# Gathering a table by one-hot matmuls: table rows folded by 2 in place of 4, and a gather queue tied to it from its first gather on

## The reference

```
x = x + relu(ln(x) @ W + segment_sum((ln(x) @ M)[src], dst))          # 200000 edges, sorted by dst
z = ln(x)
h = (z @ W_gat).reshape(N, 4 heads, 4 experts)                        # 16 numbers a node
e = leaky_relu(a_src[src2] + a_dst[dst2])                             # 131072 unsorted edges, and a loop a node
alpha = segment_softmax(e, dst2)
scores = ln(segment_sum(h[src2] * alpha, dst2) + b).mean over heads   # 4 numbers a node
w = softmax(top2(scores))
x = x + sum over experts e of w[e] * (gelu(z @ W1[e] + b1[e]) @ W2[e] + b2[e])
```

## Time and profile before

| | us |
|---|---|
| median of 3 runs | 3602.7 (3602.44 to 3619.45) |
| the profiled execution, its own time | 3607.5 |
| its span, first to last instruction | 3606.3 |
| mean granted TensorE clock in it | 0.872 of full |

### The profile page before, as it was taken

One profiled execution on the slowest core, in us unless ns is written; L12 is line 12 of the kernel. 1 busy time (PEld: TensorE's weight loads), 2 busy tenths in 40 slices (PEclk: granted clock), 3 DMA queues, 4 the chain that ended last, 5 costly groups with the idle time before them and its releaser, 6 DMA issues.

```text
span 3606.3 us, 43520 instructions
## 1 busy us (share of the span) xinstructions
PE 2660.3 (74%) x13434; PEld 1983.9 (55%) x13459; DVE 2198.0 (61%) x5820; ACT 900.2 (25%) x1563; POOL 2364.7 (66%) x2799
## 2 busy tenths in 40 slices
PE   2665767778777777777777877877777888888925
PEld 1443555555545555545555555555555767777824
DVE  6677676677775555465455555555313768787857
ACT  3000111111112222211111111111133545565513
POOL 4666666666666666656666666666888788888540
PEclk9667888879888888989989989989887999999968
DMA  9676665666666666656666666666414112222146
GB/s 289 219 253 201 184 196 183 199 201 193 191 190 205 188 197 196 197 170 200 211 195 215 199 189 215 204 203 210 114 22 120 42 40 54 53 66 52 39 146 225
DMA packets 476805, 601.23 MB, mean 167 GB/s; under 512 B 72486, under 2 KB 415390, under 8 KB 474526
## 3 DMA queue, kind: packets, MB, share of 16 engines
q1 hardware_dynamic: 378766, 375.94, 32.2%
q0 software_dynamic: 97216, 219.88, 22.2%
q10 hardware_dynamic: 592, 2.64, 0.2%
HBM read 313.06 MB, written 286.79 MB: 166 GB/s over the span
## 4 chain that ended last, share of the span: by engine, by line
PE 25%; DVE 22%; another core or an unknown queue 14%; issue 11%; DMA 2%; ACT 2%; POOL 1%; DVEq 0%; SPq 0%; ACTq 0%; POOLq 0%
PE wide L1637 7%; PE wide L1526 6%; DVE ring L834 6%; PE wide L1576 4%; PE wide L1586 4%; DVE one_hot L767 3%; DVE picked L892 2%; DMA ring<-xn_d,srci 2%; DVE low_hot L881 2%; DVE by_row L994 1%; DVE by_row L987 1%; PE wide L1545 1%; POOL ring L1729 1%; PE wide L1682 1%
## 5 line engine op out<-in xcount | busy, mean ns | idle before, releaser
L1729 POOL DMA_INDIRECT ring<-xn_d,srci x1611 | 1556.9, 966 | 913.5 <-DVE ring L834 417.2
L834 DVE SCALAR_TENSOR_TENSOR ring<-ring,same_v,wide 128x256 f32<-128x256 f32 x1610 | 771.3, 479 | 934.2 <-remote 390.7
L1526 PE MATMUL wide<-ring,one_hot 128*128 128x256 f32 x3222 | 971.4, 440 | 402.7 <-DVE ring L834 237.7
L1526 PEld LDWEIGHTS wide<-ring,one_hot 128*128 128x128 f32 x3222 | 673.6, 219 | 653.4 <-DVE ring L834 222.3
L1637 PE MATMUL wide<-tab_parts,low_hot 128*128 128x208 bf16 x6288 | 672.0, 260 | 115.3 <-issue 103.2
L1637 PEld LDWEIGHTS wide<-tab_parts,low_hot 128*128 128x128 bf16 x6288 | 565.9, 100 | 221.5 <-issue 205.0
L1780 POOL DMA_INDIRECT g<-tab_d,srt x500 | 495.4, 991 | 82.6 <-issue 45.3
L1586 PE MATMUL wide<-w2s,hh 128*128 128x256 f32 x1568 | 416.0, 413 | 45.5 <-DVE yo L808 28.1
L1576 PE MATMUL wide<-xt,w1s 128*128 128x512 f32 (+1 forms) x832 | 413.1, 625 | 7.3 <-ACT hh L1255 5.4
L1255 ACT ACTIVATE hh<-wide,b1c 128x512 f32<-128x512 f32 (+1 forms) x208 | 137.8, 662 | 1067.0 <-PE wide L1576 488.5
L1586 PEld LDWEIGHTS wide<-w2s,hh 128*128 128x128 f32 x1568 | 327.1, 210 | 117.9 <-issue 28.1
(11 more groups left out here) (370 smaller groups left out, 1881.5 us busy)
## 6 DMA issues: line engine op xcount, KB each, us to landing
run_d<-ring SPq DMA_DIRECT2D x201, 1024.0 KB
ring<-xn_d,srci POOLq DMA_INDIRECT x1611
y_d<-yo SPq DMA_DIRECT2D x196, 128.0 KB
comb<-y_d SPq DMA_DIRECT2D x28, 896.0 KB
low_row<-low_d SPq DMA_DIRECT2D x13, 1024.0 KB
sum_d<-g SPq DMA_DIRECT2D x15, 768.0 KB
g<-tab_d,srt POOLq DMA_INDIRECT x500
xn_d<-ring SPq DMA_DIRECT2D x7, 896.0 KB, 6.9
```

The source lines that it names most:

```text
L834: dve_at["run", j] = step(V.scalar_tensor_tensor(out=o, in0=ring[:, (j - 1) // JC % RING, (j - 1) % JC, :], scalar=same_v[:, j:j + 1], in1 ...
L1526: mm = T.matmul(bank[pair_bank[p]][:, j % 2 * D:(j % 2 + 1) * D], one_hot[:, j // 4 % 4, j % 4, :], ring[:, j // JC % RING, j % JC, :], st ...
L1729: G.indirect_dma_start(out=ring[:, s, j % JC, :], out_offset=None, in_=xn_d, in_offset=at_rows(srci[:, j:j + 1])).then_inc(sem(f"gather{s} ...
```

## The change

- The low part of a node number becomes 8 bits (256 rows, two halves of 128 lanes), the high part runs over 25 values (`HI` = 25). A column takes 3 parts x 2 halves = 6 matmuls of 400 = 16 x 25 table columns, into one bank of its own.
- All one-hots of the low part come from ACT: two halves a block, two instructions each of 512 columns, as many as before. `low_columns` on DVE is gone.
- `pick` takes half a block (two columns, two banks, 2 x 16 x 25 sums), so it runs twice a block, in the first and the third turn. Four halves (two blocks) can be open in PSUM; PE waits twice a block for a pick of two blocks before. The semaphore `picked` counts halves.
- `high_hot` has 25 entries a column and is an 8-bit integer.
- The lock: every gather from number 56 on waits, the first for 8 halves (4 blocks), the last for 237 (118.5 blocks).
- In the end stage a pause stands ahead of each of the second part's 28 gathers.
- SP loads a tile's register once and keeps it: for the stores of `x1_d` and `tab_d` (49 each) it uses the one that `fetch` loaded, and for `y_d` it loads with the first expert alone. PE no longer waits for `one_hot` from visit 8 on.

```diff
-    HI = -(-NT // 4)
-    LOW = 4 * P
+    HI = -(-NT // HALVES)
+    LOW = HALVES * P
+    WIDE = 4 * P
...
-    high_hot = r.take("high_hot", [P, NTC, HI], BF16)
+    high_hot = r.take("high_hot", [P, NTC, HI], U8)
...
-    low_hot = q.take("low_hot", [P, DEPTH, 4, LOW], BF16)
-    picked = q.take("picked", [P, 4, HX, HI], F32)
+    low_hot = q.take("low_hot", [P, DEPTH, HALVES, WIDE], BF16)
+    picked = q.take("picked", [P, 2, HX, HI], F32)
...
-        def low_columns(b):
-
-            c = chunk_of[b]
-            V.wait_ge(sem(f"low_in{c % 2}"), sent(c // 2))
-            if b >= DEPTH:
-                V.wait_ge(sem("picked"), b - DEPTH + 1)
-            at = block_in[b] * LOW
-            for q_ in range(4 - ACT_QUARTERS):
-                dve_at["low_hot", b] = step(V.tensor_scalar(low_hot[:, b % DEPTH, q_, :], low_row[:, c % 2, at:at + LOW],
-                                                            lane[:, q_:q_ + 1], None, ALU.is_equal))
...
+        def pick(b, h):
+            m = 2 * b + h
+            c, k = chunk_of[b], pool_cols[chunk_of[b]] + block_in[b] * 4 + 2 * h
+            V.wait_ge(sem("picked"), m + 1)
...
+            if m >= 1:
+                V.wait_ge(dve_step, dve_at["pick", (m - 1) // 2, (m - 1) % 2])
+            first = HALF_BANK[m % 4]
+            dve_at["taken", m] = then(V.tensor_tensor(
                 picked[:, :, :, :],
...
+                wide[:, first:first + 2, 0:HX * HI].rearrange("p k (f h) -> p k f h", h=HI),
+                high_hot[:, 2 * m:2 * m + 2, None, :].broadcast_to([P, 2, HX, HI]), ALU.mult))
+            dve_at["pick", b, h] = step(V.tensor_reduce(g[:, c % GR, k:k + 2, 0:HX], picked[:, :, :, :], AXX, ALU.add))
...
+        def low_half(b):
+
+            c, at = chunk_of[b], block_in[b] * WIDE
             A.wait_ge(sem(f"low_in{c % 2}"), sent(c // 2))
+            for i in range(HALVES):
+                A.activation(far_off[:, b % 2, i, :], low_row[:, c % 2, at:at + WIDE], ACT.Abs,
+                             bias=lane_n[:, i:i + 1]).then_inc(sem("far_off"), 1)
             if b >= DEPTH:
+                A.wait_ge(sem("picked"), 2 * (b - DEPTH + 1))
...
         def visit(j):
-            if j % 4 == 0:
+            if j % 4 == 0 and j < 8:
                 T.wait_ge(dve_step, dve_at["one_hot", j // 4])
...
-                            if b >= DEPTH:
-                                T.wait_ge(dve_step, dve_at["taken", b - DEPTH])
-                        at = i % 2 * (2 * P)
+                        m = 2 * b + i // 2
+                        if i % 2 == 0 and m >= 4:
+                            T.wait_ge(dve_step, dve_at["taken", m - 4])
                         for k in range(3):
-                            for q_ in range(4):
-                                mm = T.matmul(bank[BLOCK_BANK[b % DEPTH] + i // 2][:, at:at + HX * HI],
+                            for q_ in range(HALVES):
+                                mm = T.matmul(bank[HALF_BANK[m % 4] + i % 2][:, 0:HX * HI],
...
-                if before_it > left + LOCK_FREE:
-                    G.wait_ge(sem("picked"), (before_it - left - LOCK_FREE) * LOCK_BLOCKS // (sum(pool_cols) - left) + 1)
+                if before_it >= left:
+                    G.wait_ge(sem("picked"), LOCK_FIRST + (before_it - left) * LOCK_HALVES // (sum(pool_cols) - left))
...
             for t in range(t0, t1):
+                if part:
+                    pause_once()
...
-                    tile = Q.value_load(tiles_i[0:1, 0, 4 * c + k:4 * c + k + 1], min_val=0, max_val=NPAD - P)
-                    Q.dma_start(y_d[e, bass.ds(tile, P), :], yo[:, ny % 4, :]).then_inc(sem(f"y_out{ny % 4}"), 16)
+                    if e == 0:
+                        unit_rows[k] = Q.value_load(tiles_i[0:1, 0, 4 * c + k:4 * c + k + 1], min_val=0,
+                                                    max_val=NPAD - P)
+                    Q.dma_start(y_d[e, bass.ds(unit_rows[k], P), :], yo[:, ny % 4, :]).then_inc(sem(f"y_out{ny % 4}"), 16)
```

More of the change, by code:

```diff
@@ L9 @@
 I16 = mybir.dt.int16
+U8 = mybir.dt.uint8
 I32 = mybir.dt.int32
@@ L36 @@
 AHEAD = 2
-BLOCK_BANK = (4, 6, 0, 2)
+HALF_BANK = (4, 6, 0, 2)
 PAUSE = 280
-LOCK_FREE = 12
-LOCK_BLOCKS = 122
+LOCK_FIRST = 8
+LOCK_HALVES = 230
 TC = 32
 WIDE_CHUNKS = 3
-ACT_QUARTERS = 2
+HALVES = 2
 GR = 5
@@ L217, in build @@
     q = Region(r4)
-    tab_parts = q.take("tab_parts", [P, 3, 4, HX, HI], BF16)
+    tab_parts = q.take("tab_parts", [P, 3, HALVES, HX, HI], BF16)
     scored = q.take("scored", [P, TC_MAX, HX], F32)
@@ L851, in split_table @@
             left = whole
-            then(V.memset(tab_parts[:, :, :, :, NT // 4:HI], 0.0))
+            then(V.memset(tab_parts[:, :, :, :, NT // HALVES:HI], 0.0))
             for k in range(3):
@@ L856, in split_table @@
                 o = tab_parts[:, k, :, :, :].rearrange("p q f h -> p h q f")
-                full = NT // 4 * 4
-                step(V.tensor_copy(o[:, 0:NT // 4, :, :], left[:, 0:full, :].rearrange("p (h q) f -> p h q f", q=4)))
-                then(V.tensor_copy(o[:, NT // 4, 0:NT - full, :], left[:, full:NT, :]))
+                full = NT // HALVES * HALVES
+                step(V.tensor_copy(o[:, 0:NT // HALVES, :, :],
+                                   left[:, 0:full, :].rearrange("p (h q) f -> p h q f", q=HALVES)))
+                then(V.tensor_copy(o[:, NT // HALVES, 0:NT - full, :], left[:, full:NT, :]))
                 if k < 2:
-                    step(V.tensor_copy(tab_part[:, 0:full, :].rearrange("p (h q) f -> p h q f", q=4),
-                                       o[:, 0:NT // 4, :, :]))
-                    then(V.tensor_copy(tab_part[:, full:NT, :], o[:, NT // 4, 0:NT - full, :]))
+                    step(V.tensor_copy(tab_part[:, 0:full, :].rearrange("p (h q) f -> p h q f", q=HALVES),
+                                       o[:, 0:NT // HALVES, :, :]))
+                    then(V.tensor_copy(tab_part[:, full:NT, :], o[:, NT // HALVES, 0:NT - full, :]))
                     then(V.tensor_tensor(tab_rest[:, :, :], left, tab_part[:, :, :], ALU.subtract))
@@ L901, in matrix_gathers @@
                 if b >= 1:
-                    pick(b - 1)
+                    pick(b - 1, 0)
                 yield
-                if b + AHEAD < NBLOCKS:
-                    low_columns(b + AHEAD)
                 yield
+                if b >= 1:
+                    pick(b - 1, 1)
+                    dve_at["pick", b - 1] = dve_at["pick", b - 1, 1]
                 yield
@@ L1318, in copy_rows @@
                              ACT.Copy).then_inc(sem("rows_copied"), 1)
-        def low_quarter(b):
-            c, at = chunk_of[b], block_in[b] * LOW
+        def low_half(b):
+            c, at = chunk_of[b], block_in[b] * WIDE
             A.wait_ge(sem(f"low_in{c % 2}"), sent(c // 2))
-            for i in range(ACT_QUARTERS):
-                A.activation(far_off[:, b % 2, i, :], low_row[:, c % 2, at:at + LOW], ACT.Abs,
-                             bias=lane_n[:, 3 - i:4 - i]).then_inc(sem("far_off"), 1)
+            for i in range(HALVES):
+                A.activation(far_off[:, b % 2, i, :], low_row[:, c % 2, at:at + WIDE], ACT.Abs,
+                             bias=lane_n[:, i:i + 1]).then_inc(sem("far_off"), 1)
             if b >= DEPTH:
-                A.wait_ge(sem("picked"), b - DEPTH + 1)
-            for i in range(ACT_QUARTERS):
-                A.wait_ge(sem("far_off"), ACT_QUARTERS * b + i + 1)
-                A.activation(low_hot[:, b % DEPTH, 3 - i, :], far_off[:, b % 2, i, :], ACT.Relu, bias=ones[:, 0:1],
-                             scale=-1.0).then_inc(sem("low_quarter"), 1)
+                A.wait_ge(sem("picked"), 2 * (b - DEPTH + 1))
+            for i in range(HALVES):
+                A.wait_ge(sem("far_off"), HALVES * b + i + 1)
+                A.activation(low_hot[:, b % DEPTH, i, :], far_off[:, b % 2, i, :], ACT.Relu, bias=ones[:, 0:1],
+                             scale=-1.0).then_inc(sem("low_half"), 1)
         done, copies = 0, iter(())
@@ L1340, in scalar_program @@
                 for b in range(AHEAD):
-                    low_quarter(b)
+                    low_half(b)
             done += 1
             if done % 4 == 2 and done // 4 + AHEAD < NBLOCKS:
-                low_quarter(done // 4 + AHEAD)
+                low_half(done // 4 + AHEAD)
             if done in weighed_at:
@@ L1861, in mlp_units @@
         def mlp_units():
[L1862 removed]
+            ny, unit_rows = 0, {}
             for what, i, k in units:
```

37 lines of the change are left out of this document (10 added, 27 removed).

## The result

The changed kernel takes 3585.3 us (median of 20 runs, 3576.4 to 3609.2) against 3615.3 (20 runs, 3602.4 to 3630.6): a ratio on record of 0.9926, 95% interval 0.9912 to 0.9939 (the two medians alone make 0.9917). The time lies in the upper end of the range, 3490 to 3597, and near that of the first rival, 3584.

A forecast was written before the change was run, and what follows sets the result against it. No engine is full (PE 74%); PE gets too few instructions while POOL gathers. Stage -45, one-hot +6.5, pauses -15, registers -8: -61.5 us on 3607.5, 3546, so 3541 for the median; range 3490 to 3597.

The forecast's parts named there:

- the first rival: Matrix stage: PE is shut out for a share of time, so columns count, not instructions; sum -18 us, 3584; chance 0.19.
- PE's rate in the first 22 blocks: Matrix stage's start: 24 matmuls a block at 4.5 a us, 5.3 us a block (bounds 4.2 and 5.7).
- The rest of the stage: Matrix stage from block 22 on: DVE becomes the late engine, 5.7 us a block, plus 10 us of waits.
- ACT no bound: Matrix stage: ACT makes all one-hots in as many instructions as before, busy 392 of 791 us; nothing.
- The lock: POOL's gathers from number 56 on in the matrix stage: the lock holds nothing, no effect on time.
- The one-hot: High digits' one-hot in the visits (L755): grows from 7.25 to 13.8 us, uncovered; +6.5 us.
- The pauses: End stage, second part's gathers: pauses relieve DVE's slow first gating; -15 us, bounds -19 and 0.
- Registers: SP's register loads and some PE waits go; -8 us, bounds -30 and 0.
- The pick's price: DVE's multiply on 8-bit one-hots in the matrix stage costs more; at 1.85 times, 3761; chance 0.05.
- the larger gain: All engines share the shortage, so halving PE's stream frees DVE, ACT and SP too; -121 us, 3481; chance 0.13.
- the clock: Matrix stage: PE, waiting for DVE, falls to its lower clock; at 30% of the blocks, 3646; chance 0.07.

The follow-up runs named there:

- after_3: The changed kernel without any edit, measured again in a later set beside its variants; 0.9852 of the kernel before.
- second group: The other three of the five sets of follow-up runs, in which the kernel before took 3553 to 3557 us.
- first group: The first two of the five sets of follow-up runs, in which the kernel before took 3612 and 3619 us.
- half_columns: The changed kernel, but from block 2 on each matmul takes 200 of the 400 table columns; one run, no ratio given.
- lock_14: The changed kernel with the lock's first wait at 14 halves in place of 8, the last still 237; 0.9891 of the kernel before.

## Why the prediction went wrong, point by point

- *PE's rate in the first 22 blocks* is the step that failed: "I take the 4.5 a us of the stage's first 110 us: 5.3 us a block". It stood on two readings. The rate was read at a granted clock of 0.71 and taken as a number of instructions, though at one clock it is nearer to a number of columns (the stretches above). And matmuls in the units that weren't slowed were taken as proof that long ones escape; but nothing shows that PE was dry there, and 553 matmuls of 400 columns run as freely when it isn't. The runs show two states in its place. Dry, blocks 5 to 19 took 7.37 us, above my upper bound of 5.7; not dry (after_3), 4.34, near the lower. Over 22 blocks 6.83 in place of 5.3 is 34 us, nearly all that the stage lacked (-8 us in place of -45).
- *The rest of the stage* was right: 109 blocks in 632 us, where 5.7 us a block and 10 us of waits make 631; 986 ns a pick; ACT no bound; POOL done at 3364 (3350 forecast). There DVE is the bound, and the change costs 18 us against the kernel before (33 in the second group); the first blocks have to bring the gain.
- *The lock* "holds nothing". It held POOL for 0.85 us, and that ended the dry spell; with the old lock the stage was 7 us longer in the profile. That a wait of POOL helps PE stood in the prediction, as a side remark without a price.
- *The one-hot* was right: 13.80 us, POOL's wait 14.59 in place of 8.05. *The pauses*: -15 forecast, -13.3 measured in the first profile (113.0 to 99.7 us to the end) and -10.5 in the second group; seven other profiles with the same pauses took 103 to 108, so that 100 came was in part luck. *Registers*: 8 forecast; the runs show no price that is theirs.
- *The rivals.* The first, by which columns count and the sum is -18, is what the first group shows (-25.7 from profile to profile). Its time fits better than its terms: 168 us for the first 22 blocks where 150 were measured, and 621 for the others in place of 632. I gave it 0.19, because of the units. The pick's price and the larger gain didn't come. Nor did the clock: 0.98 from 2765 on with PE busy 483 of 630 us. In half_columns, with PE's work halved, it was 0.67 there (PE busy 392 of 630 us), and changed between its two levels all through. The Trainium skill, "TensorE: Matmul & The Clock Gate", section "HAM oscillation — how this bites in real kernels", tells of such a clock in a kernel whose waits are longer than the work between them, a condition that the prediction left out when it called this rival likely by that section; the trace of half_columns shows such a clock (0.67), that of this kernel doesn't (0.98). In half_columns DVE set the pace, and the blocks were no longer for it (5.80).

What stays open: why gathers slow PE at all, what decides that it falls dry, and what differed between the two groups of sets.

## What to carry to other kernels

When an engine idles with no releaser while POOL issues gathers, look for where it goes back to full rate and at what POOL did just then, before making its instructions fewer: three pauses in place of one at 13 gathers took 45 to 49 us off the stage in the first group, where the change itself had taken 8, and 41 to 45 us off that of the kernel before in the second, as much as the change there. The hint stood in the kernel before's own profile, at each hold by the lock. A rate read in such a stretch belongs to the clock and the state it was read in, so price a stage for both states and not at a rate between them. And when work is moved to the next engine, count what it costs where that engine is already full (18 us here).

## What the hardware showed that I had not expected

- PE can stay dry for over 100 us beside gathers, and not be dry beside the same gathers at the same pace (137 and 553 matmuls without a gap). A stop of POOL of about 1 us (0.83 to 0.85 us in the lock, 1.12 us of pauses) ends it from one matmul to the next, but not for good: the next dry spell began after 140 matmuls of 400 columns in lock_14 (24.9 us), after 92 of 208 in the kernel before (10.1 us).
- Dry, PE starts in bursts: five matmuls of 172 ns each 1.48 us, or four of 91 ns each 0.78 us.
- DVE shows something alike in the gating: 16 to 21 us or 26 to 40, beside the same gathers.
- The kernel before ran 1.6% faster in some sets of runs than in others, the changed one 2.3%, though a pick's instruction takes the same 986 ns. The changed kernel's stage was 50 us shorter there, as PE wasn't dry; the start of its stage was 30 to 35 us earlier too, for a reason that no run shows.
